# ScalarE instead of SyncE issues the stores of the second layer's results

## The reference

```python
    x = x + _L0_conv_ref(_gn(x), qkv_w, qkv_b, proj_w, proj_b, rel_table)
    x = x + _L1_conv_ref(_gn(x))
```

```python
        w0, w1, w2 = (1, 5, 20)
        s = box_sum(box_sum(x, 1, w0), 2, w1)
        num = box_sum(s * s, 3, w2)
        d = box_sum(box_sum(box_sum(x * x, 1, w0), 2, w1), 3, w2)
        ...
        denum = d * norm[None, :, :, None]
        return jnp.nan_to_num(num / denum, nan=FILL)
```

## Time and profile before

| | |
|---|---|
| time, median of 3 runs | 3396.27 us (3393.39 to 3396.65) |
| the profiled execution: time | 3382.73 us |
| the profiled execution: span | 3380.9 us |
| TensorE busy, span | 3166.0 us, 94% |
| VectorE busy | 2784.9 us, 82% |
| ScalarE busy | 2375.2 us, 70% |
| GpSimd busy | 2263.3 us, 67% |
| transfers issued for the stores | 512, by SyncE |

### The profile page before, as it was taken

How to read it: one execution, slowest core, us unless ns; L and a number is a source line. 1 busy time by engine, 2 the same in 40 slices (tenths; PEclk the granted TensorE clock), 3 DMA queues, 4 the chain that set the end, 5 groups by cost and what they waited for, 6 DMA issues and landing times.

```text
span 3380.9 us, 146870 instructions
## 1 busy us (share of the span) xinstructions
PE 3166.0 (94%) x60544; PEld 2620.4 (78%) x60544; DVE 2784.9 (82%) x4882; ACT 2375.2 (70%) x4705; POOL 2263.3 (67%) x2522
## 2 busy tenths in 40 slices
PE   3999999999999999999999999999999999999997
PEld 2778787887888778787778787778777777787785
DVE  4788888888888888888888888888888888888883
ACT  2567776777777777777777777777777777777764
POOL 3566666666677666677666667666667666677663
PEclk8999999999999999999999999999999999999995
DMA  3333333333333333333333333333333333332220
GB/s 74 82 89 80 87 92 77 85 89 84 87 91 84 84 93 80 84 93 81 84 93 80 87 92 81 83 93 81 85 92 81 84 92 81 86 92 71 73 63 23
DMA packets 385693, 280.20 MB, mean 83 GB/s; under 512 B 261927, under 2 KB 384904, under 8 KB 385032
## 3 DMA queue, kind: packets, MB, share of 16 engines
q1 hardware_dynamic: 385032, 270.81, 32.8%
HBM read 39.35 MB, written 38.54 MB: 23 GB/s over the span
## 4 chain that ended last, share of the span: by engine, by line
PE 47%; SPq 26%; DVE 8%; issue 6%; ACT 6%; DMA 5%; POOL 1%; DVEq 0%; ACTq 0%; POOLq 0%
SPq L317 10%; SPq L325 10%; PE pP L466 9%; PE pO L481 8%; PE pS L454 6%; DMA out<-tok_out 5%; SPq L330 5%; PE pM L555 3%; DVE T L816 3%; PE pM L549 3%; PE pM L566 3%; PE pM L504 3%; PE pM L394 2%; PE pM L388 2%; PE pM L436 2%
## 5 line engine op out<-in xcount | busy, mean ns | idle before, releaser
L1052 POOL TENSOR_TENSOR T<-T,MX 128x588 f32<-128x588 f32 x1024 | 1213.0, 1185 | 602.8 <-DVE MX L823 599.5
L816 DVE TENSOR_TENSOR T<-pS,table 128x588 f32<-128x588 f32 x1024 | 781.6, 763 | 353.8 <-PE pS L454 352.4
L663 ACT ACTIVATE P<-pP 128x588 f32<-128x588 f32 x1024 | 674.8, 659 | 258.7 <-PE pP L466 231.0
L466 PE MATMUL pP<-K,T 113*128 113x113 f32 x6144 | 789.4, 264 | 14.6 <-POOL T L1052 8.4
L823 DVE TENSOR_REDUCE MX<-T 128x12 f32<-128x588 f32 x1024 | 775.0, 757 | 17.9
L481 PE MATMUL pO<-V,P 128*49 128x18 f32 x24576 | 697.7, 198 | 46.1 <-ACT g L696 39.9
L481 PEld LDWEIGHTS pO<-V,P 128*49 128x49 f32 x24576 | 662.8, 126 | 53.0 <-ACT g L696 45.1
L466 PEld LDWEIGHTS pP<-K,T 113*128 113x128 f32 x6144 | 630.3, 143 | 71.0 <-issue 23.2
L1017 POOL TENSOR_TENSOR y<-Y 96x472 f32<-96x472 f32 x224 | 217.1, 969 | 491.6 <-ACT Y L740 491.6
L454 PE MATMUL pS<-KE,QS 128*64 128x196 bf16 (+1 forms) x8192 | 474.9, 233 | 19.8 <-DMA KE<-KS 13.5
L454 PEld LDWEIGHTS pS<-KE,QS 128*64 128x64 bf16 x8192 | 302.0, 109 | 135.4 <-issue 81.6
(11 more groups left out here) (94 smaller groups left out, 5904.0 us busy)
## 6 DMA issues: line engine op xcount, KB each, us to landing
KE<-KS SPq DMA_DIRECT2D x512, 147.0 KB
KS<-knh SPq DMA_DIRECT2D x768, 49.0 KB, 2.0
QS<-qnh SPq DMA_DIRECT2D x768, 49.0 KB
out<-tok_out SPq DMA_DIRECT2D x384, 84.0 KB
tok_in<-x SPq DMA_DIRECT2D x224, 84.0 KB
KS<-knl SPq DMA_DIRECT2D x384, 49.0 KB, 2.0
QS<-qnl SPq DMA_DIRECT2D x384, 49.0 KB
tok_in<-x SPq DMA_DIRECT2D x224, 63.0 KB
```

The costliest lines, as they stand in the source:

```text
L466: mm = pe.transpose(pP[:, c, QN * at:QN * at + QN], T[j % 4][0:QN, 2 * h:2 * h + 2, :], pick)
L663: act.activation(P32[j % 3][:, :, :].rearrange("p (c a w) q -> p c a (w q)", c=2, w=2), src, ACT.Exp).then_inc(p_made, 1)
L816: dve.tensor_tensor(T[j % 4][:, :, 0:L].rearrange("p (b h) k -> p b h k", b=2), pS[:, :, 0:HALF].rearrange("p b (h k) -> p b h k", k=L), t ...
L1052: pool.tensor_tensor(t, t, MX[j % 4][:, :].unsqueeze(2).broadcast_to([128, HEADS, L]), ALU.subtract).then_inc(shifted, 1)
```

## The change

`store` moves from SyncE's program to ScalarE's. In ScalarE's loop it stands behind `keep_squares` (`csq`) and ahead of `exponentials`, in the same slot as before (`STORE_AT`). Semaphores, buffers and transfers are the same.

```diff
@@ SyncE @@
-            def store(G):
-                m, v = divmod(G, GROUPS)
-                sp.wait_ge(out_made, G + 1)
-                for h2, (t, n, row) in store_runs(v):
-                    dst = out[m][row:row + 2 * n - 1:2, :, :].rearrange("t w c -> w t c")
-                    sp.dma_start(dst, tok_out[G % 2][SIDE * h2:SIDE * h2 + SIDE, t:t + n, :]
-                                 ).then_inc(stored[G % 2], 16)
-
@@ SyncE, loop over slots @@
                 for U in units(s, STAGE_AT - 4):
                     if U % 2:
                         stage(U // 2)
-                for G in groups(s, STORE_AT):
-                    store(G)
@@ ScalarE @@
+            def store(G):
+                m, v = divmod(G, GROUPS)
+                act.wait_ge(out_made, G + 1)
+                for h2, (t, n, row) in store_runs(v):
+                    dst = out[m][row:row + 2 * n - 1:2, :, :].rearrange("t w c -> w t c")
+                    act.dma_start(dst, tok_out[G % 2][SIDE * h2:SIDE * h2 + SIDE, t:t + n, :]
+                                 ).then_inc(stored[G % 2], 16)
+
@@ ScalarE, loop over slots @@
                 for G in groups(s, DEEP_AT):
                     keep_squares(G)
+                for G in groups(s, STORE_AT):
+                    store(G)
                 for j in steps(s - 1):
                     exponentials(j)
```

## The result

The changed kernel takes 3377.14 us (median of 5 runs, 3374.05 to 3383.22), the kernel before 3396.27 beside it (5 runs, 3389.30 to 3397.99): a ratio of 0.9949, 95% interval 0.9934 to 0.9965. It is faster, by 0.5% or 17 to 19 us. The forecast was 3421, slower. The time lies in the stated range, but on the other side of zero from the likeliest case.

A forecast was written before the change was run, and what follows sets the result against it. TensorE, busy 94%, was taken as the bound. Costs 14 + 16 + 47 = 77 us less 51.8 gave +25: profiled 3382.7 became 3408, or 3421 with 13.5 to the median; range 3366 to 3485.

The forecast's parts named there:

- the likeliest case: Sign forecast for the whole kernel: slower 0.52, against faster 0.34 and same 0.14.
- The wait goes: VectorE's waits to write `tok_out` until an earlier store landed: all 51.8 us, in 57 waits, would vanish.
- What it is worth: 51.8: Gain from the store waits on `tok_out`: priced one to one at their length, 51.8 us.
- the 13.5 us by which its profile lay under the median: Profiled execution 3382.7 us against median 3396.3; the difference was added to 3408, giving 3421.
- Issues begin with `csq`, not before and not behind it: ScalarE's store issues start once `csq` has begun, running beside its 0.49 us, with 0.58 us cover before the exponential.
- An issue in mid-staging: 0.66: Length of one ScalarE store issue while SyncE issues too: 0.66 us, the middle of 0.43 and 0.88.
- x = 0.43: x is a ScalarE issue's length while SyncE issues; 0.43 us if the engines don't disturb each other, sum -11 us.
- 14 + 16 us of the places beside `csq`: Mid-staging cost: 14 us in 64 places beside the third and fifth `csq`, 16 us in 32 beside the seventh.
- The lock on the descriptor generator: Rival of mutually exclusive ScalarE and SyncE issues: x = 0.88 us, sum +75 us, time 3471; chance 0.14.
- The slack: Lateness of the exponential beside `csq` that stays free before reaching TensorE, by the path through `rd`: 0.70 us.
- The slot without `csq`: 1.46 in each of 32, 47 us: Four issues of an image's last group, between `X` and the exponential: 0.80 + x each, 47 us together.
- The cheap rival: Issues cheap (x under 0.47) or begun earlier; all but the last group's four hide: -11 or -24 us; chance 0.34.

The follow-up runs named there:

- the third buffer: Kernel before with three `tok_out` buffers instead of two, stores still issued by SyncE: 3319.07 us against 3394.08, ratio 0.9774.

## Why the prediction was wrong in its sign

The steps, one by one:
- **The wait goes.** Right: no row of it is left, and the periods behind it are 12.2 us.
- **What it is worth: 51.8.** This step failed too: the term was too small, 75 us by the third buffer. Its length varies between executions (51.8 and 61.5 in two), and the prediction priced the length alone, though the page of before has the granted clock. It measured the worth of a wait at one of 1.26 us, where no fall followed. It also carried the 13.5 us by which its profile lay under the median over to the changed kernel as a constant. The longer of the two executions is the one with the longer waits and the lower clock, so most of such a difference goes with the waits.
- **Issues begin with `csq`, not before and not behind it.** Right, 0.01 us after its start, in every place beside a `csq`. The Trainium skill's rule (Perfetto Trace Analysis, "DVE / Act Engine Instruction"), by which ScalarE's sequencer would be ready in the wait of 0.25 us ahead of `csq`, isn't borne out by these rows.
- **An issue in mid-staging: 0.66.** This is the step that failed most clearly, and it alone turned the sign: with x = 0.43 and all else as it stood the sum was -11. The two issues took 0.89 us together, 0.43 each with 0.04 between, no more than SyncE's own median, and the staging issues stayed at 0.594. The 14 + 16 us of the places beside `csq` came out at 8. The lock on the descriptor generator that the Trainium skill states (the same page, "DMA Instruction — HWDGE"), if it lasted for a whole issue as the prediction took it, would have made them 0.88 each. These rows don't bear that out; a lock that is short against an issue would fit them. Two engines issuing together do disturb each other a little (0.89 against 0.80). A few issues take far longer, 1.55 us at most and 11 above 0.8. They are no sign of a meeting: in the kernel before, where SyncE alone issues, 51 store issues are above 0.8 and the longest took 2.15. What makes them long was not tried.
- **The slack.** Somewhat too large, 0.54 instead of 0.70. It didn't matter, since 0.33 to 0.41 were needed.
- **The slot without `csq`: 1.46 in each of 32, 47 us.** Right in place, and near in size by luck, since two errors cancel. The length is 1.07 × 32 = 34: the fourth issue does meet SyncE's first staging issue, as the prediction has it (staging from 1532.08, ScalarE's issues until 1532.35), but is not lengthened by it, and the first takes 0.33 and not 0.43. The fall of the clock, which the prediction left out, adds some 15 to 21. Measured by SyncE taking these issues back: 49.

The sum as it turned out is 8 + 49 − 75 = −18, measured −17.5 and −19; the prediction's was 14 + 16 + 47 − 51.8 = +25. (The three terms are differences between medians of these kernels, so they add up to −17.5 by themselves; that the price of the stores alone is 52 to 59 is seen again with three buffers.) Of the 43 us between them 23 are the worth of the wait, and 22 the issues beside `csq`. The cheap rival had the right mechanism: at its x = 0.43 it gives −11. That this lies within 7 us is partly luck too, since its costs were 16 us too small and its gain 23.

What stays open: why TensorE's clock falls behind some idle stretches of 1.36 us or more (10 of 26 images) and not behind others, why the waits differ by 10 us between executions of one kernel, and what makes a few issues long.

## What to carry to other kernels

When a store's queue is late and its buffer is waited for, a further buffer costs no engine anything, while another engine's queue costs that engine's sequencer: here 75 us against 18. The version that beats both kernels is the third buffer with SyncE's stores, 3319 us. If an engine must issue, count its issues per place: here two of 0.43 us beside a 0.49 us instruction fit, with 0.54 us free behind them, and four don't. Place them ahead of an idle time that is there anyway, as ahead of `X`. Price a wait of TensorE at its length and at the lower clock behind it, which windows of the trace show, and take both from more than one execution.

## What the runs showed of the hardware beyond that

- ScalarE's first issue in a place takes 0.33 us and each further one 0.41 to 0.44; beside SyncE's staging, two issues took 0.09 us longer in the median.
- TensorE idle for 1.36 us was followed by 3.5 us at a granted 0.52 in one place, 1.99 idle by some 10 us at half clock in another; with more transposes ahead, the one idle stretch of 1.58 was followed by full clock. In two executions of one program the mean clock was 0.982 and 0.973.
- The profile puts a wait down to a semaphore (`<-PE pP`) where the engine's own queue had ended last. The queue's rows beside it tell the difference.
